# A graph network kernel: x is gathered from the input instead of scattered into a table first

## What is computed

```python
# layer 0: n = 50000 nodes, 25000 edges
deg  = segment_sum(ones, dst) + 1;  dinv = rsqrt(deg)
conv(x, W, b) = segment_sum((x@W)[src] * dinv[src] * dinv[dst], dst) + dinv**2 * (x@W) + b
x0 = l2norm(conv(x, W1, b1))
f(z) = conv(l2norm(conv(z, Wf1, bf1)), Wf2, bf2) + z
k1 = f(x0); k2 = f(x0 + 0.5*k1); k3 = f(x0 + 0.5*k2); k4 = f(x0 + k3)
x1 = layernorm(x + conv(x0 + (k1 + 2*k2 + 2*k3 + k4)/6, W2, b2))
# layer 1: q, k, v of x1, a softmax of q[dst].(k[src]+e) per dst, two dense layers
out = layernorm(x1 + attention(x1, src, dst, edge_attr))
```

## Time and profile before

| | us |
|---|---|
| median of 3 runs | 8224.36 |
| lowest, highest | 8223.61, 8232.91 |
| profiled execution | 8220.47 |
| its span, first to last instruction | 8218.7 |

### The profile page before, as it was taken

The page is one execution under the profiler, slowest core; times in us unless marked ns, Lnnn a source line. Parts: engine busy times, 40 slices in busy tenths (PEclk is TensorE's granted clock), DMA queues, the critical chain, the costliest instruction groups (busy, mean ns, idle before and its releaser), DMA issues. The chain is left out here.

```text
span 8218.7 us, 161609 instructions
## 1 busy us (share of the span) xinstructions
PE 6239.8 (76%) x36634; PEld 5164.9 (63%) x36634; DVE 6059.0 (74%) x16217; ACT 3772.2 (46%) x10497; POOL 5409.8 (66%) x6036
## 2 busy tenths in 40 slices
PE   5001998899989975799998999899888665566776
PEld 2001888888888853576686677667655554555554
DVE  5311787778778779779887988898799883337887
ACT  5001775666666657672373147116522332224443
POOL 0676787778877867675586667558644665665665
PEclk8555999999999989999999999999999997678998
DMA  9643446755444446679888987997899663334442
GB/s 137 178 132 92 145 145 136 130 140 148 137 140 144 141 142 187 201 226 290 259 247 264 336 251 232 311 320 235 258 370 373 194 187 84 84 83 124 125 123 87
DMA packets 1661480, 1548.86 MB, mean 188 GB/s; under 512 B 169099, under 2 KB 1572347, under 8 KB 1660839
## 3 DMA queue, kind: packets, MB, share of 16 engines
q1 hardware_dynamic: 1234087, 961.28, 40.2%
q0 software_dynamic: 160192, 335.62, 15.3%
q10 hardware_dynamic: 266560, 244.12, 8.9%
HBM read 929.00 MB, written 611.74 MB: 187 GB/s over the span
## 5 line engine op out<-in xcount | busy, mean ns | idle before, releaser
L1241 PE MATMUL bank<-c_rows,sums_all 128*128 128x256 f32 (+1 forms) x3920 | 1322.8, 420 | 550.0 <-issue 293.2
L704 PE MATMUL bank<-wf_w,c_xt 128*128 128x256 f32 x6272 | 1618.0, 381 | 4.7 <-DVE y L1448 2.8
L1213 POOL DMA_INDIRECT c_rows<-t_tab,src_row x784 | 865.5, 1104 | 723.7 <-PE bank L1241 565.0
L1241 PEld LDWEIGHTS bank<-c_rows,sums_all 128*128 128x128 f32 x3920 | 634.4, 194 | 990.5 <-issue 548.8
L1286 ACT ACTIVATE c_xt<-bank 128x512 f32<-128x512 f32 (+1 forms) x980 | 554.8, 566 | 1447.4 <-issue 690.2
L704 PEld LDWEIGHTS bank<-wf_w,c_xt 128*128 128x128 f32 x6272 | 1134.8, 191 | 133.0 <-issue 4.4
L1383 DVE SCALAR_TENSOR_TENSOR c_rows<-bank,carry,c_rows 32x256 f32<-32x256 f32 (+1 forms) x1950 | 912.5, 468 | 257.7 <-PE bank L1241 124.8
L1213 POOL DMA_INDIRECT c_rows<-z_tab,src_row x784 | 770.1, 982 | 296.2 <-issue 187.9
L1011 DVE TENSOR_TENSOR lx_lo<-bank,lx_hi 128x512 fp32r<-128x512 f32 (+1 forms) x1000 | 657.5, 658 | 348.4 <-ACT lx_hi L956 282.9
L956 ACT ACTIVATE lx_hi<-bank 128x512 fp32r<-128x512 f32 (+1 forms) x1000 | 562.3, 568 | 569.7 <-PE bank L925 441.5
L694 PE MATMUL bank<-wf_hi,lx_hi 128*128 128x256 f32 x3200 | 710.0, 303 | 79.2 <-issue 58.8
(11 more groups left out here) (303 smaller groups left out, 15697.5 us busy)
## 6 DMA issues: line engine op xcount, KB each, us to landing
c_z<-z_tab SPq DMA_DIRECT2D x882, 256.0 KB
z_tab<-lz SPq DMA_DIRECT2D x400, 256.0 KB
t_tab<-lt SPq DMA_DIRECT2D x400, 256.0 KB
z_tab<-y ACTq DMA_DIRECT2D x392, 256.0 KB
c_own<-z_tab SPq DMA_DIRECT2D x392, 256.0 KB
t_tab<-y ACTq DMA_DIRECT2D x392, 256.0 KB
c_own<-t_tab SPq DMA_DIRECT2D x392, 256.0 KB
fl_x<-x_tab SPq DMA_DIRECT2D x396, 128.0 KB
```

The costliest lines, as they stand in the source:

```text
L704: last = nc.tensor.matmul(out, x(k), w[:, k, :], start=(k == 0), stop=(k == ks - 1 and not bias))
L1213: pool.indirect_dma_start(out=rows[:, s, i, 0:XW] if first else rows[:, s, i, :], out_offset=None, in_=source, in_offset=bass.IndirectOffs ...
L1241: nc.tensor.matmul(psum[s % 2][:, i * win:(i + 1) * win], sums[:, j * 2 + i, :], rows[:, s, i, 0:win], start=True, stop=True).then_inc(S[" ...
```

## The change

`x_tab`, its clearing and its scatter are gone, and so is `free_tab`. The second block of `prepare` finds, for each row of the 200 local tiles, which node belongs there, on PE. The alone nodes of grid column t have consecutive ranks, from a base that the running sum gives. DVE makes a one-hot of (rank mod 128) for each column (`hot_row`), and a matmul with it spreads column and partition number of the nodes over 128 rows by their rank, with 4 columns for the two tiles that they can fall into. 396 such matmuls, then 8 that add each column's result into the tile of its base (`hot_base`). What comes out is `local_node`. POOL works out `own_key`, `pos_f` and the inverse root beside it, and three small tables go to DRAM, with pairs of 4-byte values: `pos_tab` (row, inverse root) by node, `own_tab` (inverse root, node) by node or, behind NPAD, by filler rank.

In `local_pass` POOL gathers `lx_in` from the input x by `local_node`, 2 indirect DMAs in each of the turns q = 0, 2, 4, 6 of a block, and `invert` moves from lag 5 to lag 12. SP keeps a contiguous copy (`xl_tab`) from which x is read again for the last layer. `edge_tables` has now, for each edge tile, a look-up in `own_tab`, a scatter of (row, inverse root) into `pos_tab` for the node in that slot, and a gather of x from the input, and after these 196 look-ups by src. It takes a step in every slot that isn't of layer 0 (36 of 40). DVE builds the sum matrices here too (`build`), and SP's program of this pass is written out instead of looped.

The 196 look-ups by dst are put behind the gathers of the stages `end` 1, 2 (49 each) and 3 (98). Stage `first` gathers from the input by `src_i`, and takes the inverse roots from tiles that are there already, so four small instructions of DVE for each pair are gone.

```diff
-    x_tab = dram("x_tab", [NPAD + SLOTS, XW])
-    free_tab = dram("free_tab", [SLOTS, 1], I32)
+    pos_tab = dram("pos_tab", [NPAD, 2], I32)
+    own_tab = dram("own_tab", [NPAD + LATE * P, 2], I32)
+    xl_tab = dram("xl_tab", [NPAD, D])
...
-                for lo in (FILL, 0):
-                    sp.dma_start(m["x_tab"][lo:lo + SLOTS, :].rearrange("(p n) c -> p n c", p=P),
-                                 zeros[:].unsqueeze(1).to_broadcast([P, TE, XW])).then_inc(S["cleared"], 16)
...
-                sp.wait_ge(S["cleared"], 48)
...
+                for j in range(TN // 4):
+                    if j >= 2:
+                        dve.wait_ge(S["counted"], TE + 4 * (j - 1))
+                    v.tensor_tensor(hot_row[:, j % 2, :, :], cols_h[:, 0:P].unsqueeze(1).to_broadcast([P, 4, P]),
+                                    rank_lo[:, j * 4:j * 4 + 4].unsqueeze(2).to_broadcast([P, 4, P]), ALU.is_equal
+                                    ).then_inc(S["hot"], 1)
...
+                for n in range(2):
+                    for k in range(4):
+                        last = v.tensor_scalar(hot_base[:, n, k, :], cols[0:Q, :], base_of[:, n, k:k + 1], None,
+                                               ALU.is_equal)
...
+                for t in range(TN):
+                    if t % 4 == 0:
+                        pe.wait_ge(S["hot"], TE + t // 4 + 1)
+                    at = t % Q * 4
+                    nc.tensor.matmul(psum[t // Q][:, at:at + 4], hot_row[:, t // 4 % 2, t % 4, :], picks[:, t, :],
+                                     start=True, stop=True).then_inc(S["counted"], 1)
...
+                for n in range(2):
+                    for k in range(4):
+                        last = nc.tensor.matmul(psum[7][:, 0:TN], found_turned[:, n, k * P:(k + 1) * P],
+                                                hot_base[:, n, k, :], start=(n == 0 and k == 0), stop=(n == 1 and k == 3))
...
-                    for i in range(4):
-                        pool.indirect_dma_start(
-                            out=m["x_tab"], out_offset=bass.IndirectOffsetOnAxis(ap=stage_pos[:, s, i:i + 1], axis=0),
-                            in_=x_in[:, s, i, :], in_offset=None).then_inc(S["scattered%d" % s], 16)
...
+    for t in range(TE):
+        if t + 3 < TE:
+            find_own(t + 3)
+            yield
+        pool.wait_ge(S[f"own_found{t % 4}"], 16 * (t // 4 + 1))
+        pool.indirect_dma_start(out=m["pos_tab"], in_=three[:, t, 0:2], in_offset=None, out_offset=at(three[:, t, 2:3])
+                                ).then_inc(S["placed"], 16)
         yield
+        if t >= 4:
+            pool.wait_ge(S[f"xo_out{t % 4}"], 16 * (t // 4))
+        pool.indirect_dma_start(out=xo[:, t % 4, :], out_offset=None, in_=a["x"], in_offset=at(three[:, t, 2:3])
+                                ).then_inc(S[f"xo_in{t % 4}"], 16)
+        yield
...
+                def gather_x(b, q, odd):
+                    if layer[q] != 0:
+                        return
...
+                    for i in range(2):
+                        t = (b * G + group[q]) * 2 + i
+                        pool.indirect_dma_start(
+                            out=x_in[:, h, i, :], out_offset=None, in_=a["x"],
+                            in_offset=bass.IndirectOffsetOnAxis(ap=m["local_node"][:, t:t + 1], axis=0)
+                        ).then_inc(S[f"gathered{h}"], 16)
...
-                staggered(pool, blocks, Q, early, [(0, gather_own), (5, invert)], unrolled=True)
+                staggered(pool, blocks, Q, early, [(0, gather_x), (12, invert)], unrolled=True)
...
-                staggered(sp, blocks, Q, early, [(0, load), (3, load_again), (14, store_own), (16, store)])
...
+                staggered(sp, blocks, Q, early,
+                          [(0, load_rows), (3, load_again), (5, keep), (16, store), (17, store_own), (18, store_sums)],
+                          unrolled=True)
...
-                staggered(dve, blocks, Q, early, [(6, normalise), (1, low), (3, add_rest), (3, take)])
+                staggered(dve, blocks, Q, early, [(6, normalise), (1, low), (3, add_rest), (3, take), (0, build)])
...
+                for t in found_here.get(j, ()):
+                    pool.indirect_dma_start(
+                        out=m["dst_pair"][:, t, :], out_offset=None, in_=m["pos_tab"],
+                        in_offset=bass.IndirectOffsetOnAxis(ap=m["dst_i"][:, t:t + 1], axis=0),
+                        bounds_check=NPAD - 1, oob_is_err=False).then_inc(S["dst_found"], 16)
...
-                    v.tensor_copy(dinv[:, bass.ds(j * 2, 2)], own[:, s, :, D + 1])
-                    v.tensor_copy(m["node_of"][:, bass.ds(j * 2, 2)], own[:, s, :, D])
```

More of the change, by code:

```diff
@@ L249, in early @@
             m[name] = passing.enter_context(nc.sbuf_tensor(name, list(shape), dt))
-        for name in ("own_row", "src_i", "dst_i", "zero_i", "free_i", "slot_id_i"):
-            early(name, [P, TE], I32)
-        early("node_pos", [P, TN], I32)
+        early("own_key", [P, TE], I32)
+        early("own_three", [P, TE, 3], I32)
+        early("local_node", [P, TL], I32)
+        early("dst_f", [P, TE])
+        early("up", [P, P])
+        early("down", [P, P])
         for name, ks, width in (("w1", 1, H2), ("wf1", 2, H2), ("wf2", 2, H2), ("w2", 2, D)):
@@ new lines, in _ @@
+                act.wait_ge(S["pos_turned"], 12)
+                nc.scalar.activation(found_turned[:, 0, :], psum[4][0:Q, :], ACT.Copy).then_inc(S["root"], 1)
+                act.wait_ge(S["pos_turned"], 22)
+                for rows, c in ((pos_rows, 1), (own_rows, 0)):
+                    last = nc.scalar.activation(rows[:, :, :, c].bitcast(F32),
+                                                psum[5][0:Q, :].rearrange("q (k p) -> q k p", p=P), ACT.Copy)
+                last.then_inc(S["rows_set"], 1)
@@ L608, in edge_tables, with at, find_own @@
+                sp.wait_ge(S["edges_in"], 96)
+def edge_tables(nc, a, S, m, pool, xo):
+    g = nc.gpsimd
+    key, three = m["own_key"], m["own_three"]
+    def at(index):
+        return bass.IndirectOffsetOnAxis(ap=index, axis=0)
+    def find_own(t):
+        pool.indirect_dma_start(out=three[:, t, 1:3], out_offset=None, in_=m["own_tab"],
+                                in_offset=at(key[:, t:t + 1])).then_inc(S[f"own_found{t % 4}"], 16)
+    for t in range(3):
+        find_own(t)
         yield
@@ L629, in edge_tables @@
[L629 to L637 removed]
+    pool.wait_ge(S["placed"], 32 * TE)
@@ L903, in _ @@
+                for k in range(2):
+                    sp.wait_ge(S[f"s_out{k}"], 16 * (builds // 2))
                 for k in range(4):
@@ L1224, in _ @@
                 pool.wait_ge(S["c_constants"], 1)
+            found_here = {}
+            if end and r in (1, 2):
+                found_here = {j: [(r - 1) * (pairs // 2) + j // 2] for j in range(1, pairs, 2)}
+            elif end and r == 3:
+                found_here = {j: [pairs + j] for j in range(pairs)}
             for j in range(pairs + (8 if rooted else 0)):
```

462 lines of the change are left out of this document (236 added, 226 removed).

## The result

The changed kernel takes 7995.26 us, median of 4 runs (7990.16 to 8001.67), beside 8223.99 us for the kernel before (4 runs). The ratio is 0.9724, with a 95% interval of 0.971 to 0.9738: 229 us faster. The forecast was 7822 us, 402 us faster, with a range of 7680 to 8000. So the time is just inside the range, at its upper end, and 173 us of the expected gain are missing. The profiled execution has a span of 7990.4 us.

What follows compares the result with a forecast made beforehand. Bound: 781 us lie ahead of the first useful matmul, where the change works; POOL is nearly full in the local pass. 8218.7-529+5+84-8+20+30-10+6 = 7816.7 us of span, 5.7 more for the median: 7822 us, range 7680 to 8000.

Steps and rivals of the forecast that it cites:

- Ahead of the local pass: Before the local pass: clearing and scatter block removed, second block longer; -529 us, bounds -555 and -460, then +5 at its start.
- (c): Second block of `prepare`: 99 one-hots on DVE, each with four weight loads and matmuls on PE; 64 us, from 39 to 131.
- Rival D: Second block of `prepare`: one-hots paced by PE at the lower clock, + 67 us, 7889 us in all; chance 0.10.
- a local pass more than 70 us from 2209 + 131: Local pass: sign that the forecast is wrong, if its length differs from 2209 + 131 us by over 70.
- the bunch of gathers: Local pass: POOL's bunched indirect DMAs stall 21 blocks by 4 us each, +84 us (0 to 168); last three blocks -8.
- 83 of 84.9 us: Local pass: POOL's work per block in 21 blocks, 44 indirect DMAs of 1.28 us plus 26.4 us of inverse roots.
- DVE: 20 us: Local pass: building sum matrices and casts on DVE costs +20 us of the 38 that this makes at most, from 0.
- DMA: +30 us: Local pass: scatter writes to `pos_tab`, all 25,088 live, cost +30 us net, bounds -45 and +130.
- rival C: Local pass: POOL becomes the bound and the scatter costs by the write, + 80 + 100 = 8000 us; chance 0.18.
- The 45 us that the prediction counted as lost: Local pass of the kernel before: 45 us lost over the seven blocks of the scatter to `free_tab`.
- `first`: Runge-Kutta stage: DVE freed of four instructions per pair, but POOL fills the pair too; -10 us, from -30 to 0.
- The look-ups by dst: Stages `end`: 196 look-ups cost POOL nothing but take time of full DMA engines, 0.08 us each; +6 us, 0 to 16.

Runs made afterwards that it cites:

- version with 32 steps: Kernel with SP's `store_own` at lag 26, POOL's table steps left out in all eight turns q = 0 to 7, SP's stores behind POOL's issue: 7743.76 us, ratio 0.9362.
- third set: Last of three sets of four kernels, the kernel before beside it at 8271.73 us; the changed kernel took 8052.68 us, without look-ups by dst 7978.88 us.

## Why the prediction was right, and where it was wrong

**Ahead of the local pass: right.** -533 against -524. The clearing's wait is gone. The one-hots (c) run at 0.60 us each, paced by DVE, and PE has 0.34 us to spare in each. The group and PE's timeline show both:

```profile
L484 DVE TENSOR_TENSOR hot_row<-cols_h,rank_lo 128x512 f16<-128x512 f16 x99 | 60.2, 682 | 0.0
```

```profile
156.68 0.27 PE L578 MATMUL bank<-picks,hot_row 128*128 128x4 f16 x4 [0.34 <-DVE hot_row L484]
```

The group has 682 ns for one, close to the f32 row of as many elements that the term leaned on, 658 ns. The Trainium skill ("VectorE: DVE Perf Modes", Mode 2x_1P) would have it so for a source repeated along the row, and the trace agrees. Rival D fell by its price: at a granted clock of 0.50 four loads with their matmuls took 0.27 us, where D had put 1.32. A load took 107 ns at this clock, against 97 at 1.00, and not twice as much. The block ended at 231, where 232 was put, the split of the weights took 5 us less, and the start of the pass 3 us more than before where 5 were put.

**The local pass: the failed step.** The prediction itself named what would show it wrong: a local pass more than 70 us from 2209 + 131. It took 2458, 118 us over. The prediction said of the order only that `invert` at lag 12 makes nothing later by itself. It followed POOL's queue and not SP's. Two moves stood in the diff, the gather of `lxo` into the table steps and `store_own` from ahead of `store` to behind it, and no sentence asked in which turn SP would come to the wait and in which POOL would issue what it waits for. That missing term is the largest of the pass: 2458 - 2216 = 242 us (235 within one set), shown by moving it away (0.946) and by putting it into the kernel before (1.0225).

**The other terms of the pass.** POOL: 84 - 8 = 76 us were put on the bunch of gathers. Both edits of POOL's steps together take 2216 - 2165 = 51 us off the pass, or 78 by the differences within the sets, so the size was fair. But the reason was largely wrong: one DMA per turn gained nothing over two, and it is mostly POOL's total that costs. The prediction had this total, 83 of 84.9 us, and charged nothing for it, only the bunch; a DMA more costs 1.06 to 1.13 us. DVE: 20 us were put and 0 measured, since DVE has slack where POOL paces. DMA: +30 us were put for the 8-byte writes, and beside a look-up they cost 0. The Trainium skill ("DMA: Bandwidth & Descriptors", Specifications) has transfers under 512 B done as read-modify-write, which rival C built on. The traces agree in so far as the writes took more DMA time than reads of as many bytes (10.0% against 7.9%). In the time of the pass no price is to be seen at this load, and the measurement decides. What remains is 2165 - 2207 = -42 us. The 45 us that the prediction counted as lost to the scatter to `free_tab` went with it, and should have stood as a gain: a block takes 83 to 105 us there before, and 82 to 88 in the version with 32 steps. This last figure compares two sets and is worked out, not shown, and why the one scatter cost PE time and the other doesn't is open.

**The stages behind.** `first` gained 0 and not 10 us: POOL's two gathers and root still fill the pair. The look-ups by dst were put at 6 us (0 to 16) from a row of the local pass. The stages that hold them came out 51 us longer, of which some 8 are not theirs. The look-ups cost 71 us in the third set and 5 in the first, all of it in `end` 3. The step that failed is the price of one transfer, taken from a stretch with a DMA share of 0.5. That full DMA engines are the mechanism is not shown, as with engines as full the price was once nothing.

**Why the range held.** 7822 + 242 (SP) - 25 (POOL) - 20 (DVE) - 72 (DMA) + 45 (look-ups) + 10 (`first`) - 9 (ahead) is 7993, which is the median within 3 us. That it closes proves little, since the -72 is what was left over in the pass once the other terms were taken. The range reached to 8000 for rival C, POOL as the bound and a scatter paid by the write. Of that POOL as the bound is half true. The rest of the loss was in SP's order, which no term or rival had, and that it ended 5 us inside the range is luck.

## What to carry to other kernels

When a step is moved from one place of an engine's program to another, write down for each pair of signal and wait in which turn each is reached in real time, on both engines, and count the DMA queue as an engine. A store that waits for a late gather holds back every store behind it. A total of waits says little: ask whether the longest is longer than what stands behind can bear. And POOL was full here at 82 to 84% busy, since 0.2 to 0.3 us of idle time stand ahead of each indirect DMA: test whether there is room by adding one more of them, not by the busy share. When kernels are measured on different occasions, put one kernel without a change beside each, and distrust a difference of a stage that is no larger than that kernel's own.

## What was not expected of the hardware

- One more indirect DMA cost 1.06 to 1.16 us where POOL was full, whether it read or wrote 8 bytes a row. A scatter took 0.18 us more of all 16 DMA engines than a look-up, which at a DMA share of 0.54 cost no time.
- At a granted clock of 0.50, the lower of TensorE's two levels (1.2 GHz), four f16 weight loads of 128 x 128, each with a matmul of 4 columns, took 0.27 us together. In the window at 1100 of the local pass the granted clock was 0.81 with PE busy 61 of 80 us, and 0.96 with PE busy 75.
- Some stages changed between sets of runs with their code unchanged: the attention took 533 to 625 us up to its first scatter, and 49 look-ups beside full DMA engines cost 0 to 30 us.
